# Attention heads with queries and keys in scaled 16-bit parts, the head's factor moved into the row maximum, and new step tables

## The reference

```python
# block 1: attention, 16 heads of 128
qkv = (x @ w_qkv.T).reshape(B, S, 3 * H, D)          # D = 128
logits = einsum('bqhd,bkhd->bhqk', q, k) * D ** -0.5
weights = softmax(logits)                            # over 1024 keys
out = einsum('bhqk,bkhd->bqhd', weights, v).reshape(B, S, H * D) @ w_out.T
# block 2: feed-forward with ternary weights, 256 -> 1024 -> 256, silu gate
# block 3: causal attention with a latent of 64, 16 heads of 16
# block 4: feed-forward with weights lut[idx], 256 -> 688 -> 256, silu gate
```

## Time and profile before

| | |
|---|---|
| median of 3 runs | 897.76 us (896.94 to 898.62) |
| the profiled execution, its own time | 896.64 us |
| its span, first to last instruction | 894.9 us |
| mean granted TensorE clock | 0.995 |
| heads, about | 0 to 590 us |
| feed-forward 0, latent attention, feed-forward 1 | 590 to 650, 650 to 840, 840 to 895 us |

### The profile page before, as it was taken

The page is one execution under the profiler, slowest core; times in us unless marked ns, Lnnn a source line. Parts: engine busy times, 40 slices in busy tenths (PEclk is TensorE's granted clock), DMA queues, the critical chain, the costliest instruction groups (busy, mean ns, idle before and its releaser), DMA issues. The chain is left out here.

```text
span 894.9 us, 13229 instructions
## 1 busy us (share of the span) xinstructions
PE 834.4 (93%) x4405; PEld 537.4 (60%) x4406; DVE 766.2 (86%) x1595; ACT 607.9 (68%) x1044; POOL 429.6 (48%) x456
## 2 busy tenths in 40 slices
PE   8889999999999989999998999989868999999997
PEld 3555665566566556566555666567754555554686
DVE  3788999899989999999999999766699796886647
ACT  5677767777788677776776777855565767758632
POOL 4134354444454448678679765142242354444301
PEclk9999999999999999999999999999989999999999
DMA  3487769958887677777766777630000000000001
GB/s 126 85 183 155 149 103 188 181 114 154 172 154 157 131 133 147 149 140 134 162 120 118 130 141 141 119 110 1 1 0 1 1 1 1 1 1 2 1 1 48
DMA packets 276868, 86.31 MB, mean 96 GB/s; under 512 B 267584, under 2 KB 272448, under 8 KB 276416
## 3 DMA queue, kind: packets, MB, share of 16 engines
q1 hardware_dynamic: 275520, 80.05, 45.9%
q0 software_dynamic: 992, 5.34, 2.2%
q10 hardware_dynamic: 288, 0.07, 0.0%
HBM read 17.29 MB, written 1.05 MB: 20 GB/s over the span
## 5 line engine op out<-in xcount | busy, mean ns | idle before, releaser
L1433 ACT ACTIVATE EP<-ps,rinv 128x1024 f16<-128x1024 f32 x128 | 142.3, 1113 | 46.7 <-DVE rinv L1671 42.9
L1676 DVE SCALAR_TENSOR_TENSOR EP<-ps,rinv,EP 128x1024 f16<-128x1024 f32 x128 | 163.3, 1276 | 3.8 <-ACT EP L1433 3.3
L1423 ACT ACTIVATE ps<-ps,nmax 128x1024 f32<-128x1024 f32 x128 | 139.2, 1088 | 34.8 <-DVE nmax L1661 34.3
L1661 DVE TENSOR_REDUCE nmax<-ps 128x1 f32<-128x1024 f32 x128 | 155.0, 1211 | 0.8 <-PE ps L1002 0.8
L1000 PE MATMUL ps<-KH,QH 128*128 128x512 f32 x256 | 115.3, 451 | 7.0 <-DVE KL L1643 4.2
L2018 POOL TENSOR_TENSOR wgu<-wgu,ptm 128x688 f32<-128x688 f32 x60 | 99.7, 1662 | 42.7 <-DVE ptm L1775 40.6
L1000 PE MATMUL ps<-ET,VH 128*128 128x512 f16 x256 | 97.2, 380 | 9.1 <-DMA ET<-EP 5.3
L2018 POOL TENSOR_TENSOR wdn<-wdn,ptm 128x512 f32<-128x512 f32 x45 | 57.7, 1283 | 92.0 <-DVE ptm L1775 90.8
L1002 PE MATMUL ps<-KH,QL 128*128 128x512 f32 x256 | 100.8, 394 | 0.0
L1001 PE MATMUL ps<-KL,QH 128*128 128x512 f32 x256 | 100.4, 392 | 0.0
L1002 PE MATMUL ps<-ET,VL 128*128 128x512 f16 x256 | 97.0, 379 | 0.0
(11 more groups left out here) (253 smaller groups left out, 2142.1 us busy)
## 6 DMA issues: line engine op xcount, KB each, us to landing
wqr<-in_wqk SPq DMA_DIRECT2D x16, 256.0 KB, 3.4
wgu<-in_tern POOLq DMA_DIRECT2D x3, 1024.0 KB, 6.7
wvr<-in_wv SPq DMA_DIRECT2D x8, 256.0 KB, 4.0
wor<-in_wo SPq DMA_DIRECT2D x16, 128.0 KB, 3.2
ET<-EP SPq DMA_TRANSPOSE x128, 4.3
X<-in_x SPq DMA_DIRECT2D x2, 512.0 KB, 5.7
prw<-in_down_idx POOLq DMA_DIRECT2D x2, 256.0 KB, 8.0
tern<-in_l_wuq_rep SPq DMA_DIRECT2D x1, 512.0 KB, 4.3
```

The costliest lines, as they stand in the source:

```text
L1423: e.activation(bank, bank, ACT.Exp, bias=nmax[:, c:c + 1], scale=1.0, accum_out=rsum[:, c:c + 1]).then_inc(exped.sem, 1)
L1433: e.mul(EP[:, n % NE_RING, 0, :], SB(u, j), rinv[:, c:c + 1]).then_inc(e_hi.sem, 1)
L1661: e.tensor_reduce(nmax[:, c:c + 1], SB(u, j), AX.X, ALU.max, negate=True).then_inc(maxed.sem, 1)
L1676: e.scalar_tensor_tensor(out=EP[:, n % NE_RING, 1, :], in0=SB(u, j), scalar=rinv[:, c:c + 1], in1=EP[:, n % NE_RING, 0, :], op0=ALU.mult, ...
```

## The change

- `Q16`, `QR16`, `K16`, `KR16` in float16 take the place of `QH`, `QL`, `KH`, `KL` in the heads. `qk_hi` and `qk_lo` multiply by the constant `QK_DOWN = 2**-11`, no longer by a per-partition column, and they no longer wait for it (`q_back`).
- The head's factor (query by key, with 1/sqrt(128) and a minus sign) is one column `UNIT(h)`. `max` becomes one `tensor_tensor_reduce`. It reads the scores in PSUM, multiplies them by `UNIT(h)`, adds a column of zeros that is broadcast, writes the 1024 results back over the scores, and gives their minimum to `nmax`. `exp` then has `scale=-1.0`.
- `UNIT(h)` comes from two small GpSimd instructions (`q_part`, then `q_unit`), in a step of its own, `scale_wqk`.
- The squares, norm and scale steps take a number of heads. In the opening they run for head 0 and head 1 apart; later for two heads together, as before.
- A new opening table. SyncE issues the first half of x, the weights of heads 0 and 1, and then the second half of x. GpSimd issues the index tables later. `N_WARM[0]` is 24 for 46. The transposes of the opening take PSUM banks 0 to 3.
- New tables for FFN0, LATENT and FFN1. They hold the same steps in another order.

```diff
-N_WARM = (46, 30)
+N_WARM = (24, 30)
+QK_DOWN = 2.0 ** -11
...
-    before = ("W0 t0 t1 n0 n1 n2 n3 k0 K0 n4 n5 n6 T0 Q0 v0 n7 T1 X0 x0 y0 Q1 X1 y1 X2 y2 x1 x2 x3 e0 v1 h0 S0 M0 "
+    before = ("W0 k0 n0 t0 n1 g0 n2 Q0 K0 t1 n3 T0 v0 n5 n4 X0 n6 n7 y0 x0 T1 g1 x1 k1 x2 X1 X2 Q1 y1 K1 y2 x3 S0 "
...
-            for i in range(2):
-                e.dma_start(X[:, 4 * i:4 * i + 4, :], x_v[:, 4 * i:4 * i + 4, :]).then_inc(x_in[i].sem, 16)
+            e.dma_start(X[:, 0:4, :], x_v[:, 0:4, :]).then_inc(x_in[0].sem, 16)
             for h in range(2):
                 e.dma_start(wqr[:, h, :, :], a["wqk"][:, h, :, :]).then_inc(wqk_in[h].sem, 16)
+            e.dma_start(X[:, 4:8, :], x_v[:, 4:8, :]).then_inc(x_in[1].sem, 16)
...
-                        mm = three(SB(u, j)[:, cs], QH[:, b, qs], QL[:, b, qs], KH[:, b, cs], KL[:, b, cs], True, True)
+                        mm = three(SB(u, j)[:, cs], Q16[:, b, qs], QR16[:, b, qs], K16[:, b, cs], KR16[:, b, cs], True, True)
...
-                    w.wait_ge(*q_back[h - h % 2, which])
-                    e.mul((QH, KH)[which][:, h % 2, cs], bank, UNIT(h, which)).then_inc(qkv_hi.sem, 1)
+                    e.mul((Q16, K16)[which][:, h % 2, cs], bank, QK_DOWN).then_inc(qkv_hi.sem, 1)
...
-                    e.activation(bank, bank, ACT.Exp, bias=nmax[:, c:c + 1], scale=1.0,
+                    e.activation(bank, bank, ACT.Exp, bias=nmax[:, c:c + 1], scale=-1.0,
...
-                    e.scalar_tensor_tensor(out=lo[:, h % 2, cs], in0=bank, scalar=UNIT(h, which),
-                                           in1=f32(hi[:, h % 2, cs]), op0=ALU.mult,
-                                           op1=ALU.subtract).then_inc(qkv_lo.sem, 1)
+                    e.scalar_tensor_tensor(out=lo[:, h % 2, cs], in0=bank, scalar=QK_DOWN, in1=hi[:, h % 2, cs],
+                                           op0=ALU.mult, op1=ALU.subtract).then_inc(qkv_lo.sem, 1)
...
-                    e.tensor_reduce(nmax[:, c:c + 1], SB(u, j), AX.X, ALU.max,
-                                    negate=True).then_inc(maxed.sem, 1)
+                    h = unit(u)[0]
+                    w.wait_ge(*q_back[h])
+                    w.wait_ge(*filler_set[1])
+                    e.tensor_tensor_reduce(SB(u, j), SB(u, j), zero[:, :].broadcast_to([P, 1024]), UNIT(h), 3.0e38,
+                                           ALU.add, ALU.min, nmax[:, c:c + 1]).then_inc(maxed.sem, 1)
...
+                    e.tensor_scalar(q_part[:, i0 // 2:i1 // 2], wpow[:, i0:i1:2], -SCALE0 * 2.0 ** 106, None,
+                                    ALU.mult).then_inc(q_part_set.sem, 1)
+                    w.wait_ge(*q_part_set[h0])
+                    e.tensor_tensor(q_unit[:, o:o + n], q_part[:, i0 // 2:i1 // 2], wpow[:, i0 + 1:i1:2],
+                                    ALU.mult).then_inc(q_back.sem, 1)
...
-        s2042 d02 l10 o24 o25 d03 @latent s2062 l00 s2142 o26 z2 o27 p010 s2162 p000 i25 p110 p100 m010 m000 m120
+        d02 s2042 l10 o25 o24 d03 @latent s2062 s2142 l00 p010 o26 o27 p000 s2162 i24 p110 m120 m100 p100 m030 m110
```

More of the change, by code:

```diff
@@ L126, in order_of_heads @@
             todo.append(("turn_in", 0, j))
[L127 to L130, removed]
+        elif what in "kKg":
+            todo.append(({"k": "square_wqk", "K": "norm_wqk", "g": "scale_wqk"}[what], j, 1))
+        elif what == "I":
+            todo.append(("load_index", j))
         elif what == "Q":
@@ L198, in order_of_heads @@
                 loads = []
-            for kind, ahead in weights.get((r, step), []):
+            for kind, ahead, *n in weights.get((r, step), []):
                 if h2 + ahead < H0:
-                    todo.append((kind, h2 + ahead))
+                    todo.append((kind, h2 + ahead, *n))
                     if kind in after and h2 + ahead + after[kind][1] < H0:
@@ L297, in build @@
         ident = sbuf(top, "ident", [P, P])
+        with ExitStack() as ctx:
+            Q16, QR16, K16, KR16 = (sbuf(ctx, n, [P, 2, 1024], F16) for n in ("Q16", "QR16", "K16", "KR16"))
         QH, QL, KH, KL = (sbuf(top, n, [P, 2, 1024], F32R) for n in ("QH", "QL", "KH", "KL"))
@@ L390, in build, with UNIT @@
         dn0 = TU[2].rearrange("p (e n) -> p e n", e=8)
-        def UNIT(h, which):
-            i = 4 * (h // 2 % 2) + 2 * (h % 2) + which
+        def UNIT(h):
+            i = 2 * (h // 2 % 2) + h % 2
             return q_unit[:, i:i + 1]
@@ L556, in build @@
         filler_set.mark(0)
+        filler_set.mark(1)
         ones_in.mark(0)
@@ L609, in build @@
             elif what == "square_wqk":
-                for i in range(4):
-                    q_squared.mark(*at, i)
+                for h in range(at[0], sum(at)):
+                    q_squared.mark(h, 0)
+                    q_squared.mark(h, 1)
             elif what == "norm_wqk":
-                q_normed.mark(*at)
-                q_norm.mark(*at)
-                q_power.mark(*at)
-                q_factor.mark(*at)
-                q_scaled.mark(*at)
-                q_scaled.mark(at[0] + 1)
-                for i in range(2):
-                    q_back.mark(*at, i)
+                for x in (q_normed, q_norm, q_power, q_factor):
+                    x.mark(sum(at) - 1)
+                    x.at[at[0],] = x.n
+            elif what == "scale_wqk":
+                for h in range(at[0], sum(at)):
+                    q_scaled.mark(h)
+                q_part_set.mark(at[0])
+                q_back.mark(sum(at) - 1)
+                q_back.at[at[0],] = q_back.n
             elif what == "square_wv":
@@ L691, in build @@
             elif what == "norm_wqk":
-                take_work(step, q_norm[at])
+                take_work(step, q_norm[at[0]])
             elif what == "norm_wv":
@@ L1637, in _ @@
                     bank, cs = ps[:, WB + BANK[("qk", *at)][0], :], slice(half * 512, half * 512 + 512)
-                    hi, lo = ((QH, QL), (KH, KL))[which]
-                    w.wait_ge(*q_back[h - h % 2, which])
+                    hi, lo = ((Q16, QR16), (K16, KR16))[which]
                     w.wait_ge(*qkv_hi[("qk", *at)])
```

149 lines of the change are left out of this document (79 added, 70 removed).

## The result

The changed kernel takes 882.51 us (median of 4 runs, 881.14 to 883.33), the kernel before on the same chip 897.39 us. The ratio is 0.9831 with an interval of 0.9814 to 0.9848: 15.2 us less. The profiled execution takes 882.52 us, its span is 880.7. I had forecast 891, and 883 to 899 as the range. The sign was right. I had forecast 6.8 us of gain, less than half of the 15.2 measured. One of the twelve executions of h1 took 2078.86 us, and its median and ratio leave it out.

What follows compares the result with a forecast made beforehand. The heads were taken as paced by TensorE in the first half and VectorE in the second. Heads -1.5, opening -2.8 and tables -2.2 us made -6.5 from 896.64: 890.1, predicted as 891 for the median, range 883 to 899.

Steps and rivals of the forecast that it cites:

- What bounds the heads; TensorE's parts: Heads: TensorE paces the first half, VectorE the second; 16-bit score matmuls save 0.086 us per tile, counted as -4.1 us.
- VectorE's maximum: Heads: the write-back row maximum costs 1.20 us for 1.13, +0.07 us per tile; the first half has room for it.
- The rival with an uncovered read: Heads: accumulator read not covered, a maximum costs 1.34 us, VectorE bounds all heads: 916 us; chance 0.12 with milder cases.
- The residuals: Heads: the 64 low-part splits of queries and keys fall from 744 to 685 ns, -3.8 us in all on VectorE.
- The sum in the heads: Heads: -4.1 us in the first half and +2.6 in the second, together -1.5 us, bounds -11 and +5.
- The opening: Start of the kernel: first product 3.7 us earlier, first scores at about 21.5 us; -2.8 us, bounds -4 and 0.
- The clock rival: Opening: a pause behind the shorter filler loses the clock, opening -0.8 us, heads and tables 0: 897 us; chance 0.13.
- The first two terms behind the heads: Behind the heads: wait of 1.70 us at the down product covered, -1.7 us; wait of 4.30 for the queries' split, -0.5.
- The step that failed: From 655 to 895 us: the hundreds of moved steps counted as 0, between -5 and +4 us.
- The rival at 883: Whole kernel: TensorE's relief comes through in both halves, -8 us in the heads, -3 and -4 besides: 883; chance 0.18.

Runs made afterwards that it cites:

- h1: The kernel before with steps 1 to 47 of the new LATENT table, the steps left in the old order: 897.9 us, ratio 0.9998.
- e6: The kernel before with only the 16-bit parts of queries and keys, the factor and its column still at the split: 896.4 us, ratio 0.9970.
- e5: The kernel before with only the new write-back row maximum: 904.5 us, ratio 1.0044.
- e1: The changed kernel with the old tables for FFN0, LATENT and FFN1: 894.6 us, ratio 0.9946 to the kernel before.
- e3: The kernel before with only the new FFN0 table: 898.0 us, ratio 0.9990.
- h3: The kernel before with steps 1 to 391 of the new LATENT table, up to behind the last row maximum, and the old tail: 888.3 us, ratio 0.9885.
- a2: The kernel before with only LATENT steps 217 to about 275 in the new order: 898.7 us, ratio 1.0002.
- e7: The changed kernel with 36 filler matmuls for 24: 886.1 us, ratio 0.9862 to the kernel before.
- e2: The kernel before with the three new tables (FFN0, LATENT, FFN1) alone: 887.1 us, ratio 0.9853.
- e4: The kernel before with only the new LATENT table: 888.7 us, ratio 0.9885.
- h2: The kernel before with steps 1 to 200 of the new LATENT table, the steps left in the old order: 895.2 us, ratio 0.9959.
- a1: The kernel before with only LATENT steps 205 to 391 in the new order: 894.2 us, ratio 0.9963.
- e8: The changed kernel with the old opening (order table, load order, 46 fillers, both heads' squares together): 886.3 us, ratio 0.9862 to the kernel before.

## Why the prediction was too small

- **What bounds the heads; TensorE's parts.** Right in kind: most of it in the first half, little in the second (-1.2 and -0.4 in e6's markers). The size was less than the -4.1 for the first half. The pitch of 0.216 came as said, but TensorE's waits for VectorE's splits of queries and keys grew from 10.5 us in the heads to 14.7 in e6 and ate part of it.
- **VectorE's maximum.** The cost was right: 1278 ns and a pitch of 1.20 us (median of the maxima), the read covered. The rival with an uncovered read fell. The total of e5, +4.0 us for +4.5, fits better than the account of it. The second half gave +3.4 for +4.5, and the first half +2.7 where the prediction counted nothing: the 0.31 us per tile in which VectorE was idle did not take up 0.07 us more. TensorE's waits for the splits of queries and keys grew there too, from 10.5 us in all the heads to 14.2.
- **The residuals.** The length was right, 685 ns. What it gives in time no run shows by itself.
- **The sum in the heads.** -2.2 and +1.3 in the traces against -4.1 and +2.6; together -0.9 for -1.5. Both halves were counted at twice their size, and the errors cancel. That the sum came out is luck.
- **The opening.** -2.8 forecast, -2.8 measured (0.7 to 4.9), and the traces say that the agreement is partly luck: the first scores came 1.1 us earlier than before, the first `OH` 1.6. Inside it the first product came at 14.50 as worked out. The clock rival's event happened too, behind a pause of 1.27 us where I had expected about 3: six products at the lower level and the first scores at 23.13 for 21.5. The Trainium skill, "TensorE: Matmul & The Clock Gate", "Part 1: The HAM clock gate", has the throttled state as the default, released by activity. The traces agree: the 0.50 stands behind pauses of 1.27 and 1.50 us, and with the pauses filled it is gone.
- **All of it up to here** was forecast at -4.3 and is -4.8 by e1 (-6.6 to -3.1), with the reservations above.
- **The first two terms behind the heads.** The waits of 1.70 and 4.30 us fell as read. By the markers the FFN0 table gives 1.8 us up to the first latent maximum, for 1.7 forecast. The start of LATENT gives 1.6 there for 0.5, and 0.2 to 0.8 at the 17th maximum, so VectorE does give much of it back. The times of e3 and h1 (-0.9 us, -2.3 to +0.6, and -0.2, -1.0 to +0.7) resolve neither.
- **The step that failed**: "The hundreds of moved steps from 655 to 895 us cannot be summed from rows; I count 0, between -5 and +4." Steps 48 to 391 of LATENT gave 10.1 us (h3 less h1), 7.8 of them between the 65th and the 192nd maximum in the traces. The lower bound of -5 had no row behind it. A row that was there: TensorE was idle for 12.6 of 182.4 us, and from 640 to 840 us VectorE waited for TensorE for 12.7 us in all. These are two engines that take turns in waiting, and a bound of -12.6 would have held the result. It is no strict bound, since 3.8 of the 7.0 us that the changed kernel gained there came out of time in which TensorE is recorded as busy. Which of the moved steps do it stays open. a2 shows that it isn't the largest wait by itself.
- **The rival at 883.** Its time came out, and its mechanism did not: it had -8 in the heads, -3 for the opening and -4 for the tables, where the runs have about -1, -3 and -10.

## What to carry to other kernels

When an order table is replaced, don't put its effect at nothing because the steps can't be summed. Take the idle time of the busiest engine in that stretch as a first estimate of the room (12.6 us here, of which some 10 were gained), and look for two engines that wait for each other by turns: windows in which one is full and the other short, followed by the reverse. One such wait removed alone only moves (a2). Compare traces by markers in the program: here three of the five stretches repeat within 0.4 us, where the times of the kernel before spread over 5. Don't take an engine's mean idle time as room that covers new work (e5). A filler that keeps the clock up must not stand ahead of a small matmul on which a chain waits (e7). Splitting it around that and filling the pauses kept the clock up in the opening, and its gain was not carried through the heads.

## What the runs showed of the hardware

- A per-partition column in place of a constant costs the two-operand vector operation 59 ns (744 to 685 at 512 columns) with float16 out. With fp32r out the column has 744 too, and the two splits without a column in the kernel before (`KW`) have 683.
- A maximum that writes 1024 results back to PSUM costs 0.07 us more pitch than a plain reduction, 1.20 for 1.13 (medians), since its accumulator read overlaps the next instruction.
- The clock in the old opening is not settled by the program. In the earlier trace rows the first product comes at 18.11 us, and it and those behind it run at a pitch of 0.22. In e2, whose opening is the same code, it comes at 17.86, and soon the pitch is 0.43:

```profile
17.86 0.39 PE L1000 MATMUL ps<-xh,wqh 128*128 128x512 f16 x1 [0.98 <-DVE xl L1604]
...
18.86 0.63 PE L1000 MATMUL ps<-xh,wqh 128*128 128x512 f16 x1
19.29 0.63 PE L1001 MATMUL ps<-xl,wqh 128*128 128x512 f16 x1
```

The first scores then start at 25.17 us for 24.27. What TensorE did ahead of it differs: its first pause among the transposes was 1.29 us in e2 and 0.97 before. Twelve traces have the old opening. In the seven with 0.97 to 1.02 us in that pause (before, e4, h1, h2, h3, a1, a2) all products run at 0.22. In four of the five with 1.15 to 1.62 us (e2, e3, e5, e8) the pitch goes to 0.43; in e6, with 1.24, it does not. So the longer pause goes with the lower clock, and it isn't all of the cause.
